# Hybrid transformer block on one core: first turns of the feed-forward and both ends of the second attention regrouped

## The reference

```python
x = x + attention_a(layernorm(x))   # 32 heads of width 2, sparse top-51 mask from a pairwise network
x = x + ffn(layernorm(x))
x = x + attention_b(layernorm(x))
x = x + ffn(layernorm(x))           # same weights as the first

# ffn
gate, up = split(h @ w_gate_up.T)   # each 2048 wide
out = (silu(gate) * up) @ w_down.T

# attention_b, 16 heads
q1, k1, q2, k2, v = split(x @ W_attn)
lam = exp(lq1 . lk1) - exp(lq2 . lk2) + LAMBDA_INIT
score = softmax(q1 k1' * scale - lam * q2 k2' * scale)
out = (1 - LAMBDA_INIT) * (score @ v) @ W_proj
```

## Time and profile before

| | |
|---|---|
| median of 3 runs | 3274.63 us (3268.64 to 3274.65) |
| profiled execution | 3272.49 us, span 3271.1 us |
| granted TensorE clock, mean | 0.973 |
| busy: TensorE, VectorE, ScalarE, GpSimd | 94%, 65%, 47%, 18% |
| first feed-forward | from 1600 to 2152.9 us |
| second attention | from 2152.9 to 2717.9 us |
| second feed-forward | from 2717.9 us to the end |

### The profile page before, as it was taken

The page is one execution under the profiler, slowest core; times in us unless marked ns, Lnnn a source line. Parts: engine busy times, 40 slices in busy tenths (PEclk is TensorE's granted clock), DMA queues, the critical chain, the costliest instruction groups (busy, mean ns, idle before and its releaser), DMA issues.

```text
span 3271.1 us, 44270 instructions
## 1 busy us (share of the span) xinstructions
PE 3081.4 (94%) x17041; PEld 1741.7 (53%) x17041; DVE 2134.0 (65%) x4098; ACT 1549.3 (47%) x2512; POOL 574.7 (18%) x423
## 2 busy tenths in 40 slices
PE   6999999999999799999799999978899888999999
PEld 3434334334333344444388888843444335888887
DVE  6988998998899777775344444444766765444443
ACT  4988888888888266666411111013343342111110
POOL 1000000000000635351110001003454441001000
PEclk9999999999999699999899999998999998999999
DMA  2000000000000000000110000033332312000001
GB/s 72 2 1 11 1 1 11 1 1 11 1 2 1 1 1 2 1 1 2 58 39 20 20 20 1 1 99 95 84 96 66 97 33 77 20 20 22 17 1 52
DMA packets 32278, 86.95 MB, mean 27 GB/s; under 512 B 7171, under 2 KB 7172, under 8 KB 29637
## 3 DMA queue, kind: packets, MB, share of 16 engines
q1 hardware_dynamic: 29446, 83.43, 8.6%
q10 hardware_dynamic: 2624, 0.69, 0.1%
HBM read 59.60 MB, written 20.97 MB: 25 GB/s over the span
## 4 chain that ended last, share of the span: by engine, by line
PE 41%; DVE 3%; DMA 3%; POOL 2%; issue 1%; ACT 1%; SPq 0%; POOLq 0%; DVEq 0%; ACTq 0%
PE ps L1114 21%; PE ps L1128 10%; PE ps L1473 3%; PE ps L1537 2%; POOL ex_sum L1441 2%; DMA k_stack<-halves 1%; PE ps L1504 1%; PE ps L1489 1%; PE ps L1461 1%; PE ps L1515 1%; DMA halves<-lo_b 1%; DVE out_t L1586 0%; DMA ffn_raw<-in_w_ffn 0%; PE ps L1096 0%; PE ps L1526 0%
## 5 line engine op out<-in xcount | busy, mean ns | idle before, releaser
L628 DVE TENSOR_SCALAR pair_in<-key_words,row_words 128x512 f32<-128x512 f32 x1792 | 726.3, 481 | 44.1 <-PE ps L515 40.1
L713 ACT ACTIVATE pair_mid<-ps,row_bias 128x512 f32<-128x512 f32 x896 | 588.1, 688 | 133.3 <-PE ps L515 116.0
L515 PE MATMUL ps<-pair_in,w_hi 128*64 128x512 f16 x3584 | 584.3, 390 | 8.6 <-DVE pair_in L628 8.5
L1192 ACT ACTIVATE ffn_silu<-ps 128x512 f32<-128x512 f32 x128 | 76.2, 595 | 829.2 <-PE ps L1114 829.2
L1155 DVE TENSOR_TENSOR ffn_inner<-ffn_silu,ps 128x512 f32<-128x512 f32 x128 | 88.0, 687 | 565.5 <-PE ps L1114 565.5
L923 DVE TENSOR_REDUCE maxes<-ps 128x2 f32<-128x1024 f32 x256 | 308.6, 1224 | 110.4 <-PE ps L860 108.9
L515 PEld LDWEIGHTS ps<-pair_in,w_hi 128*64 128x64 f16 x3584 | 202.4, 108 | 301.5 <-issue 67.0
L967 ACT ACTIVATE ex<-ps 128x512 f32<-128x512 f32 x512 | 295.5, 597 | 131.0 <-PE ps L879 113.6
L515 PE MATMUL ps<-pair_in,w_lo 128*64 128x512 f16 x1792 | 352.3, 388 | 0.0
L1114 PE MATMUL ps<-ffn_z_hi,ffn_w_hi 128*128 128x512 f32 x1024 | 276.8, 392 | 7.6 <-DVE ffn_z_lo L1147 7.6
L1114 PE MATMUL ps<-ffn_z_lo,ffn_w_hi 128*128 128x512 f32 x1024 | 277.1, 393 | 0.0
(11 more groups left out here) (190 smaller groups left out, 4327.3 us busy)
## 6 DMA issues: line engine op xcount, KB each, us to landing
ffn_raw<-in_w_ffn SPq DMA_DIRECT2D x16, 1536.0 KB, 6.7
q_stack<-halves SPq DMA_DIRECT2D x48, 256.0 KB, 5.1
k_stack<-halves SPq DMA_DIRECT2D x48, 256.0 KB, 5.9
halves<-hi_b SPq DMA_DIRECT2D x16, 512.0 KB, 2.6
halves<-lo_b SPq DMA_DIRECT2D x16, 512.0 KB, 3.6
out<-x SPq DMA_DIRECT2D x4, 1024.0 KB, 4.3
x<-in_x SPq DMA_DIRECT2D x6, 512.0 KB, 5.9
wb_qk<-in_wb_qk SPq DMA_DIRECT2D x1, 2048.0 KB, 8.0
```

The costliest lines, as they stand in the source:

```text
L515: s = nc.tensor.matmul(ps[F2 * half:F2 * half + F2, bank + which, :], w_part[:, :], words.rearrange("p (s two) -> p s two", two=2)[:, :, o ...
L628: s = nc.vector.tensor_scalar(p.pair_in[:, (4 * n + i) % N_PAIR, :], p.key_words[:, b % 2, :], p.row_words[:, b % 2, row:row + 1], None, A ...
L713: nc.scalar.activation(p.pair_mid[:, n % NG, which, :], ps[:, bank + which, :], ACT.Relu, bias=bias).then_inc(p.mid_made, 1)
```

## The change

- `load_root`, new, sends one square root of a column to an unused tile on ScalarE, after each of the first three stages.
- Feed-forward: "turned" does one slice per step; batch 0 uses four banks (6, 7, 4, 5); the first chunk comes in three DMAs, with a semaphore for each part, and its splits lie between the turns; the next batch's scaling is sent a step earlier; "up" is one step for gate and one for up, and each multiplication waits only for its own operands; all four turns of the next batch lie in the first output tile of "up".
- Second attention, head: the row of ones waits for the scaled tiles of batch 0; half a product goes ahead of "query_scale", which moves to bank 5; units 0 and 1 are multiplied and sent ahead of the loop, unit 2 at the start of unit 0; two of the four value tiles of batch 0 move into the loop, ahead of batch 1's turns. From unit 2 on the order is as before.
- Second attention, end: in the last unit VectorE adds the exponentials of heads 0 and 1 and GpSimd those of heads 2 and 3. The last batch's projections are divided: three quarters ("early_b") for tiles 0, 1, 2 before "weighted" 3, before "sums" and after it, and for tile 3 after the first "last_b"; "last_b" does the last quarter and the addition to x. They use banks 0 to 3.

```diff
+def load_root(k):
+    k.act.wait_ge(k.pool_setup, IDENT_READY)
+    k.nc.scalar.activation(k.root_unused[:, :], k.ident[:, 0:1], ACT.Sqrt)
...
 def order_of_feed_forward():
-    order = [("load", 0), ("load", 1), ("split", 0), ("norm", 0), ("turned", 0, 0), ("turned", 0, 1)]
+    order = [("load", 0), ("load", 1), ("norm", 0), ("turned", 0, 0), ("turned", 0, 1), ("split", 0, 0),
+             ("turned", 0, 2), ("turned", 0, 3), ("split", 0, 1), ("split", 0, 2), ("norm", 1)]
...
             for o in range(OC):
-                order.append(("up", c, b, o))
-                if first:
-                    order.append(("turned", b + 1, o))
+                for g in range(2):
+                    order.append(("up", c, b, o, g))
+                    if c == 0 and b + 1 < B and o == 0:
+                        order += [("turned", b + 1, 2 * g), ("turned", b + 1, 2 * g + 1)]
+                        if g and b + 2 < B:
+                            order.append(("norm", b + 2))
...
+        def turn_bank(b, f):
+            return 6 + f % 2 if b else (6, 7, 4, 5)[f]
...
+                for n, (z_part, w_part, z_part_made, w_part_made) in enumerate((
+                        (z_hi, w_hi, z_hi_made, w_hi_made), (z_lo, w_hi, z_lo_made, w_hi_made),
+                        (z_hi, w_lo, z_hi_made, w_lo_made))):
+                    for f in range(ND):
+                        pe.wait_ge(z_part_made, ND * b + f + 1)
+                        pe.wait_ge(w_part_made, 3 * c + f // 2 + 1)
...
+                if c == 0:
+                    for part, (first, end) in enumerate(PARTS):
+                        nc.sync.dma_start(raw[:, 0, first:end], d["w_ffn"][0][:, first:end]).then_inc(
+                            first_loaded[part], 16)
...
 def order_of_attention_b():
...
+            if n == UNITS - 1:
+                divisions.clear()
+                last = iter([("divide_b", n, piece) for piece in range(2 * NT)])
+                order.extend([("early_b", 2), next(last), next(last), next(last), next(last)])
+                for t in range(NT):
+                    order.append(("last_b", t))
+                    order.extend([("early_b", 3)] if t == 0 else [("stats_b", B - 1, t - 1)])
+                    order.extend(step for step in (next(last, None), next(last, None)) if step)
+                order.append(("stats_b", B - 1, NT - 1))
...
+    side += query_key_steps(0)
+    advance()
     order.append(("query_scale",))
-    side += query_key_steps(0)
+    side += query_key_steps(1)
     while side or half_done:
         advance()
-    side, due = due, []
+    side, due = due[:NT // 2], due[NT // 2:]
...
-            share = (ND, 0, NT // 2, NT // 2)[n % UNITS_B]
-            query_key = query_key_steps(n + 1) if n + 1 < UNITS else []
+            share = (ND, 0, NT // 2, NT // 2)[n % UNITS_B] + (NT // 2 if n == 0 else 0)
+            if n < 2:
+                side, query_key = query_key_steps(2)[:3 * (n == 0)] + side, []
+            else:
+                query_key = query_key_steps(n + 1) if n + 1 < UNITS else []
...
+                if step[1:] == (UNITS - 1, NT - 1):
+                    order += [("early_b", 0), step, ("early_b", 1)]
...
+        pool.wait_ge(zb_made, NT)
         nc.gpsimd.memset(k_stack[96:97, :, :, :].bitcast(F32), 1.0).then_inc(ones_made, 1)
...
+            elif kind == "early_b":
+                t, = at
+                pe.wait_ge(divided, 2 * NT * (UNITS - 1))
...
+                for c in range(ND - 1):
+                    nc.tensor.matmul(ps[:, LAST_BANKS[t], :], out_t[:, c, t * P:t * P + P], w_proj[:, c, :], start=c == 0,
+                                     stop=False)
...
-            elif kind == "exp_b" and at[0] == UNITS - 1:
-                add_exponentials(dve, nc.vector, ex_added_last, *at)
+            elif kind == "exp_b" and at[0] == UNITS - 1 and at[2] < HU // 2:
+                add_exponentials(dve, nc.vector, ex_added_last, *at, HU // 2, 0)
```

More of the change, by code:

```diff
@@ L1050, in order_of_feed_forward @@
             if b == 0 and c + 1 < CHUNKS:
-                order.append(("split", c + 1))
+                order += [("split", c + 1, part) for part in range(3)]
                 if c + 2 < CHUNKS:
@@ L1067, in feed_forward @@
     loaded = [signal("loaded_even"), signal("loaded_odd")]
+    first_loaded = [signal(f"first_loaded{part}") for part in range(3)]
     var_made, sd_made, z_made, z_turned, z_hi_made, z_lo_made = (
@@ L1436, in add_exponentials @@
                 return
-            before = (TILES - HU) * (n if n < UNITS - 1 else 0) + HU * (t - 1) + g
             if t > 1:
-                queue.wait_ge(done, before + 1 - HU)
+                queue.wait_ge(done, before + heads * (t - 2) + g % heads + 1)
             first = ex[:, tile_at(n, 0, g) % N_EX, :] if t == 1 else ex_sum[:, g, :]
@@ L1650, in gpsimd @@
         def gpsimd(kind, *at):
[L1651 to L1652 removed]
+            if kind == "exp_b" and (at[0] < UNITS - 1 or at[2] >= HU // 2):
+                n = at[0]
+                add_exponentials(pool, nc.gpsimd, ex_added, *at, HU if n < UNITS - 1 else HU // 2, (TILES - HU) * n)
         def sync(kind, *at):
```

148 lines of the change are left out of this document (74 added, 74 removed).

## The result

The changed kernel takes 3240.94 us (median of 5 runs, 3239.56 to 3241.17), the kernel before 3274.65 in the same comparison (5 runs, 3268.64 to 3277.73). The ratio is 0.9896, 95% interval 0.9885 to 0.9907: 33.7 us or 1.0% less. The profiled execution has a span of 3238.3 us (3271.1 before), at a mean granted clock of 0.978 (0.973 before).

The account below looks back on a forecast made before the run. TensorE was taken as busy nearly throughout, so only its waits or slow stretches could pay. Feed-forward starts 10.0, attention head and first units 22.3 and end 1.0 sum to 33.3 us: median 3241.3, forecast 3241, range 3231 to 3255.

Parts of the forecast that it names:

- Feed-forward starts: Start of both feed-forwards: earlier first multiplications, then a wait for the second batch's scaling; saves 5.0 us each, 10.0 together.
- the root: Three stage starts: square root's table loaded ahead in ScalarE's idle time, 1.28 us off each, counted within the starts' savings.
- Head of the attention: Second attention before its units: later memset, early root load and first product ahead of the query scale save 8.0 us.
- First two units: Second attention, units 0 and 1: waits for stacks go, one for maximum rows comes; 37.7 for 49.73 us, 12.0 saved.
- (a): Less everywhere: maximum rows queue behind unit 2's stacks, feed-forward starts give 3 each, unit 2 starts slow; 3252 us, chance 0.12.
- Unit 2: Second attention, unit 2: starts without the slow clock that followed the 5.33 us wait; 2.3 us saved.
- Last unit: End of the second attention: most projection work runs earlier, VectorE then bounds; saving 0.7, rounded to 1 us.
- (f): Last unit: VectorE's six adds each wait for a GpSimd add; 3.7 us more ahead of the sums, 3245, chance 0.18.
- (b): More: no second-batch stall or clock fall, early projections find divisions done, head at 8.9; 41 us saved, 3233, chance 0.12.
- (c): Second attention: stacks only reach the third unit late, 12 of 14.3 us in the units come back; 3253, chance 0.12.
- (d): Slower: clock falls at unit 1 and the row stall to 1.2 GHz and stays; 3275 to some 3285 us, chance 0.03.
- (e): No effect: stacks late, feed-forward starts give only the table load, end and head give less; 5.6 us saved, 3269, chance 0.02.

Follow-up runs that it names:

- e5: Changed kernel with the second batch scaled right after the first and turned before the first multiplication, in both feed-forwards: 3229.92 us.
- e1: Changed kernel with the feed-forward alone as before (its order, banks, single weight load), the early root load kept: 3255.32 us.
- e10: Changed kernel without its three early loads of the root's table: 3245.85 us.
- e9: Changed kernel without the wait ahead of GpSimd's one-row memset in the second attention: 3248.47 us.
- e3: Changed kernel with the second attention's end (last unit and projections) as before: 3241.12 us.
- e2: Changed kernel with the order of the second attention's head and first units as before, later memset and roots kept: 3259.62 us.
- e6: Changed kernel with two of the first batch's four value products moved from unit 0 to unit 1 in the second attention: 3245.28 us.
- e7: Changed kernel with the last unit's sums before the early projections and all divisions before the projection: 3235.93 us.

## Why the prediction was right

Forecast 3241 in 3231 to 3255, measured 3240.94. By its own steps, in spans: 33.3 forecast, 32.8 measured. The mechanisms of the large terms hold. That the median is met to well under 1 us is luck: the head gave 0.7 more and the end 1.1 less than forecast, the units in between gave 0.4 that I had not counted, and the same attention code took up to 8.9 us more in another profile.

- *Feed-forward starts.* 10.0 forecast, 5.05 + 4.64 = 9.7 measured. The mechanism stands: first multiplications early, then a wait for the second batch's scaling held by GpSimd (2.6 forecast, 2.50 in the trace), then the slow clock. e5 takes wait and slow clock away and gains 7.2 and 7.5, so this was the largest thing the change had left. What failed is a part of the step: I counted 1.28 of each 5.0 for the root. e1 shows it worth nothing in the old order, since the weights' landing set the start. In the new order it moves the second batch's turns by 1.27 (e10), so there it is part of the gain, but only together with the regrouping.
- *Head of the attention.* 8.0 forecast, 8.73 measured. The memset gives 4.0 (e9; 4.34 counted), root and memset together 5.82 (5.6 counted), the order 2.9. The first product starts 8.30 after the variances, 8.2 by the forecast, with 1.29 of idle time ahead of it for the 1.1 I had. The 0.7 lies behind it: from the first product to the first maximum it is 22.6 instead of 23.4, inside the bounds that I had left for the clock (7.2 and 8.9).
- *First two units.* 37.7 forecast, 37.88 measured, out of three parts. Unit 0 up to the turning of its maxima: 21.1 forecast, 21.05. From there to the first exponentials: 4.1 + 2.7 forecast, 6.24 measured. The wait for the rows is 3.95 where I took 2.7 inside bounds of 2 and 7, but the maxima ran beside the rows' way and not ahead of the wait. From there to unit 2: 8.8 and 1.0 for the clock forecast, 10.59 measured. So two misses, 0.6 less and 0.8 more, cancel. The condition of rival (a), rows behind unit 2's stacks, holds: they landed in 3.6 instead of 1.8. Against it I had written that stacks and rows hardly overlap by my times. That was a wrong reading of my own sum, which has the rows sent from about 2206 on and the stacks in near 2211. The Trainium skill (Trainium Kernel Development and Optimization, Key Constraints) says that DMAs issued from SyncE's, ScalarE's and GpSimd's queues run on the same 16 engines and interleave. The rows' 3.6 us agree.
- *Unit 2.* 2.3 forecast, 2.46 measured.
- *Last unit.* 1.0 forecast, 0.7 lost against e3 and 0.1 against the kernel before. The failed step is the time at which the last sums end. By the forecast it is 11.2 us after the last scores (2703.4 less 2692.19), in the trace 12.9. Of these 1.7 us, 1.3 are the start of the first early projection: it waits for the divisions of unit 14 and starts 3.63 after the last scores, where the sum had 2.3. Behind the sums VectorE's balance held: 13.4 us from its first reciprocal to the variances, 13.7 forecast; only ScalarE's copy of the sums, 0.7, was not counted.
- *The rivals.* (f) falls: the adds are held once in six, for 1.07 us. The Trainium skill (SBUF — State Buffer, Who interferes with whom) says that a VectorE instruction with two SBUF inputs contends with a GpSimd instruction that reads SBUF, under an exclusive lock. The add of 1.75 us agrees: it began 0.1 us behind a GpSimd add. But pairs that seldom meet make little of it. (b) nearly came true in one part of four, the head at 8.73 for its 8.9. (c) falls with the row of 2245.15, (d) with the third unit's clock of 1.00, (e) with e1 and e2. (a) was right in its mechanism for the rows and off in size.

## What to carry over

Measure what stands between a stage's last result and its first multiplication on every queue, and give the first place to what TensorE needs next: here a memset, an order of turns and the sends of two units gave 33 us, and scaling one batch earlier 11 more by the median. A wait is not a saving until one asks which wait ends next: e1 (the root behind the weights), e6 (the row wait) and e9 (1.29, of which 0.65 was the weights' own) each show one behind which another stood. Where a stage's own length wanders by 5 to 9 us, compare marks inside it between which the code is the same.

## What was not expected

- The same attention code took 541.58, 545.84 and 550.51 us in three profiles. The clock fell at different places: the first products took 1.95 us for four behind a wait of 1.29, and 3.66 behind 1.47 in e1, but 1.96 in e7 behind the same 1.47. The length of the wait alone does not tell whether the clock falls.
- A spell of low clock at unit 14's sums was there in five of the ten profiles that have the changed kernel's code at this place, each with 1.93 or 1.94 us for the eight sums: 23.3 to 23.9 us up to the last scores, where four others took 20.9 (and the tenth 21.66). So it goes with 2.4 to 3.0 us of a run. What brings it on, no run shows.
- A slow clock seems to cost nothing where TensorE waits afterwards anyway. In e10 the second batch's turns started 1.27 us later and the stage ended 0.4 later. That is one profile, in a stage that wanders by 1.5.
